# A software-pipelined transformer block: the second half's split moved into the next batch's feed-forward, the attention plan starting 16 slots ahead of it, 13 buffers in the ring, 12 filler matmuls a batch

## The reference

```
x = x + attention(layernorm(x))            # 8 heads of 16, two relative biases, causal mask over time
t = x                                      # residual for the feed-forward
n = layernorm(t)
p = softmax(n @ Wg); top = two largest, divided by their sum
for i in range(2):                         # both of the two weights
    w = n * top[..., i]
    h = gelu(einsum('btd,edf->ebtf', w, W1) + b1)
    out = out + einsum('ebtf,efd->btd', h, W2) + sum(b2)
x = t + out
```

## Time and profile before

| | |
|---|---|
| time, median of 3 runs | 2374.73 us (2370.79 to 2376.21) |
| the profiled execution | 2375.36 us |
| its span, from the first to the last instruction | 2373.6 us |
| TensorE busy (matmul) | 2212.2 us, 93% of the span |
| ScalarE busy | 1615.2 us, 68% |
| VectorE busy | 1309.2 us, 55% |
| GpSimd busy | 1063.1 us, 45% |
| mean granted clock of TensorE | 0.969 of 2.4 GHz |

### The profile page before, as it was taken

How to read it: one execution, slowest core, us unless ns; L and a number is a source line. 1 busy time by engine, 2 the same in 40 slices (tenths; PEclk the granted TensorE clock), 3 DMA queues, 4 the chain that set the end, 5 groups by cost and what they waited for, 6 DMA issues and landing times.

```text
span 2373.6 us, 48113 instructions
## 1 busy us (share of the span) xinstructions
PE 2212.2 (93%) x18213; PEld 2028.0 (85%) x18213; DVE 1309.2 (55%) x3191; ACT 1615.2 (68%) x2730; POOL 1063.1 (45%) x1051
## 2 busy tenths in 40 slices
PE   3779999999999999999998999999999999999998
PEld 2569898898988889898997988889898898988898
DVE  6246454755546466454755546466454755546453
ACT  2447677576776757677576776857677576776876
POOL 5124344443445344344443444344344443444366
PEclk7789999999999999999999999999999999999999
DMA  3412030220402212030220402212030220402200
GB/s 47 92 31 38 8 46 13 36 30 11 51 9 32 30 29 38 8 48 12 36 30 11 52 11 30 30 29 37 8 48 12 36 30 11 52 11 30 30 5 8
DMA packets 68528, 68.68 MB, mean 29 GB/s; under 512 B 20286, under 2 KB 53962, under 8 KB 68298
## 3 DMA queue, kind: packets, MB, share of 16 engines
q1 hardware_dynamic: 67634, 65.34, 19.4%
q10 hardware_dynamic: 664, 0.27, 0.0%
HBM read 10.83 MB, written 6.29 MB: 7 GB/s over the span
## 4 chain that ended last, share of the span: by engine, by line
PE 67%; DVE 17%; ACT 9%; issue 5%; POOL 1%; SPq 1%; DMA 0%; ACTq 0%; DVEq 0%; POOLq 0%
PE acc L925 20%; DVE maxes L682 7%; PE zps L914 6%; PE wide L857 6%; ACT z L535 6%; PE zps L916 6%; PE zps L915 6%; PE wide L845 5%; PE wide L828 4%; DVE h L745 3%; PE wide L871 2%; PE wide L879 2%; PE wide L864 2%; PE acc L902 2%; PE wide L811 1%
## 5 line engine op out<-in xcount | busy, mean ns | idle before, releaser
L469 POOL TENSOR_TENSOR h<-h 128x384 f32<-128x384 f32 x1024 | 1022.3, 1008 | 1236.3 <-ACT h L561 1225.6
L560 ACT ACTIVATE h<-zps,b_col 128x384 f32<-128x384 f32 x1024 | 591.6, 578 | 405.6 <-DVE h L745 346.7
L745 DVE TENSOR_TENSOR h<-zps,ratio_b 128x384 f32<-128x384 f32 x1024 | 542.3, 552 | 539.7 <-PE zps L916 528.5
L925 PE MATMUL acc<-w,h 128*128 128x128 f32 x6144 | 821.2, 277 | 0.2 <-DVE outt L754 0.2
L925 PEld LDWEIGHTS acc<-w,h 128*128 128x128 f32 x6144 | 800.5, 193 | 3.8 <-issue 0.5
L561 ACT ACTIVATE h<-h,b_col 128x384 f32<-128x384 f32 x1024 | 621.4, 607 | 0.0
L682 DVE TENSOR_REDUCE maxes<-wide 128x1 f32<-128x128 f32 (+5 forms) x768 | 430.2, 615 | 295.1 <-PE wide L828 293.6
L914 PE MATMUL zps<-x_hi,w_lo 128*128 128x384 f32 x1024 | 388.6, 379 | 11.5 <-ACT h L560 10.2
L535 ACT ACTIVATE z<-wide 128x896 f32<-128x896 f32 (+2 forms) x384 | 335.1, 916 | 33.9 <-PE wide L845 25.9
L915 PE MATMUL zps<-x_lo,w_hi 128*128 128x384 f32 x1024 | 347.9, 340 | 0.0
L916 PE MATMUL zps<-x_hi,w_hi 128*128 128x384 f32 x1024 | 347.1, 339 | 0.0
(11 more groups left out here) (99 smaller groups left out, 1469.3 us busy)
## 6 DMA issues: line engine op xcount, KB each, us to landing
stack<-halves SPq DMA_DIRECT2D x384, 96.0 KB, 3.1
stack<-halves SPq DMA_DIRECT2D x384, 24.0 KB, 2.6
out_dram<-outt SPq DMA_DIRECT2D x256, 24.0 KB, 1.6
x_in<-in_x SPq DMA_DIRECT2D x124, 48.0 KB, 2.4
stack<-max_rows SPq DMA_DIRECT2D x128, 3.0 KB
stack<-max_rows SPq DMA_DIRECT2D x128, 1.5 KB
w<-in_L_ffn_W SPq DMA_DIRECT2D x8, 256.0 KB, 4.0
stack<-z SPq DMA_DIRECT2D x2, 180.0 KB
```

What stands on the lines that cost most here:

```text
L469: pool.tensor_tensor(h1[:, PLACE[m], :], h0[:, m % 2, :], h1[:, PLACE[m], :], ALU.add).then_inc(hsum_ready, 1)
L560: act.activation(h0[:, m % 2, :], zps[BANK[m]][:, 0:CT], ACT.Gelu, bias=b1_col[:, j:j + 1]).then_inc(h0_ready, 1)
L745: vec.tensor_tensor(h1[:, PLACE[m], :], zps[BANK[m]][:, 0:CT], ratio_b[:, c * CT:(c + 1) * CT], ALU.mult).then_inc(z1_ready, 1)
L925: ins = pe.matmul(acc[:, n * P:(n + 1) * P], h1[:, PLACE[k], n * P:(n + 1) * P], w2[:, j, :], start=(j == 0 and n == 0), stop=(j == UNITS_ ...
```

## The change

The steps move earlier against the feed-forward, by 2.5 slots (the first scores) to 10.5 (the second group's first scores); the first, `stats`, goes from slot -6.5 to -16.5. So most steps stand elsewhere beside the units. The split of the second chunk is taken out of the list's end: the tokens of the second chunk are kept in a buffer of their own (`xn_last`), and their split is put at slot 15.5 of the batch that uses them, ahead of its second chunk's first unit. The ring `h1` has 13 places where it had 10; room for it comes from `mixed`, which now lies in `z`, and `outt`, which is gone (the sum is formed in `res`). The fillers are 2 and 4 at each group's first scores, and none at the split: 12 a batch. The first and the last batch get `FIRSTS` of their own, and the steps of batch 1 that would stand ahead of batch 0's slots are squeezed into its slots 0 to 9.5. The two heads of a pair share one block of ones in `val`, which makes it a quarter smaller.

```diff
-LAG = 4
-RING = 10
-FIRSTS = (2, 2, 1, 0, 1, 3, 0, 1, 2, 1, 2, 0, 2, 0, 2, 1, 0, 1, 1, 2, 0, 0, 0, 0, 0, 0, 0, 2, 3, 3, 0, 0,
-          1, 2, 1, 2, 2, 1, 0, 1, 3, 1, 0, 0, 0, 0, 2, 2, 3, 0, 1, 3, 1, 0, 0, 1, 0, 1, 0, 0, 0, 2, 0, 2)
+LAG = 5
+FIRST_LAG = 5
+KNOTS = ((-4.950000000000001, 3.0), (9.5, 9.5))
+RESIDUAL_AT = 14
+RING = 13
+FIRSTS = (2, 1, 1, 2, 2, 0, 1, 3, 1, 0, 2, 2, 0, 1, 2, 1, 0, 0, 0, 0, 0, 1, 2, 3, 1, 1, 1, 1, 1, 3, 1, 3,
+          0, 0, 0, 0, 0, 0, 2, 2, 3, 3, 1, 1, 0, 2, 0, 1, 1, 0, 0, 0, 0, 0, 0, 0, 0, 2, 0, 2, 1, 2, 1, 1)
...
-      ("split", 0): 60.0, ("split", 1): 60.0}
+AT = {("stats", 0): -16.5, ("seed", 0): -12.5, ("root", 0): -10.0, ("scale", 0): -7.0, ("turn", 0): -6.5, ("query", 0): -4.0,
+      ("key", 0): -4.0, ("value", 0): -2.5, ("rows", 0): 13.5, ("split", 1): 15.5, ("mix", 0): 23.0, ("sums", 0): 31.0,
...
                     for i in range(TILES):
-                        ins = vec.tensor_scalar(xn[:, i, :], xs[:, i, :], moments[:, 1, i, 0:1], ln_t[:, 1, i:i + 1],
+                        to = xn[:, i, :] if i < HT else xn_last[:, i - HT, :]
+                        ins = vec.tensor_scalar(to, xs[:, i, :], moments[:, 1, i, 0:1], ln_t[:, 1, i:i + 1],
                                                 ALU.subtract, ALU.mult)
...
+                if r.b > 0:
+                    vec.wait_ge(out_stored, r.at(16 * TPT * CHUNKS, 16 * (TPT * (c + 1 - CHUNKS) + 1)))
...
+                    if hh == 0 and part == 0 and (g == 1 or r.b > 0):
+                        n = WIDE["divide", 1 - g]
+                        act.wait_ge(wide_free[n % 2], r.at(WPB, n // 2 + 1 - (WPB if g == 0 else 0)))
...
                     if hh == 0 and part == 0:
-                        idle(w[:, 0:P], 3)
+                        idle(w[:, 0:P], 2)
...
                     if hh == 0 and part == 1:
-                        idle(acc[:, CT:CT + P], 5, start=False)
+                        idle(acc[:, CT:CT + P], 4, start=False)
...
                 elif step == "split":
-                    if a == 0:
-                        idle(w[:, 0:P], 8)
-                    pe.wait_ge(xn_ready, r.at(4, 3 + a))
+                    pe.wait_ge(weighed, Round(r.b - a).at(2, 1 + a))
```

More of the change, by code:

```diff
@@ new lines @@
+FIRSTS_LAST = (1, 1, 1, 1, 1, 1, 1, 1, 1, 1, 1, 1, 1, 1, 1, 1, 1, 1, 1, 1, 1, 1, 1, 1, 1, 1, 1, 1, 1, 1, 1, 1,
+          1, 1, 1, 1, 1, 1, 1, 1, 1, 1, 1, 1, 1, 1, 1, 1, 1, 1, 1, 1, 1, 1, 1, 1, 1, 1, 1, 0, 0, 0, 0, 0)
+RESIDUAL_AT = 14
+RING = 13
+FIRSTS = (2, 1, 1, 2, 2, 0, 1, 3, 1, 0, 2, 2, 0, 1, 2, 1, 0, 0, 0, 0, 0, 1, 2, 3, 1, 1, 1, 1, 1, 3, 1, 3,
+          0, 0, 0, 0, 0, 0, 2, 2, 3, 3, 1, 1, 0, 2, 0, 1, 1, 0, 0, 0, 0, 0, 0, 0, 0, 2, 0, 2, 1, 2, 1, 1)
+AT = {("stats", 0): -16.5, ("seed", 0): -12.5, ("root", 0): -10.0, ("scale", 0): -7.0, ("turn", 0): -6.5, ("query", 0): -4.0,
+      ("key", 0): -4.0, ("value", 0): -2.5, ("rows", 0): 13.5, ("split", 1): 15.5, ("mix", 0): 23.0, ("sums", 0): 31.0,
+      ("rows", 1): 31.0, ("divide", 0): 31.5, ("mix", 1): 38.5, ("sums", 1): 40.0, ("divide", 1): 41.0, ("project", 0): 41.5,
+      ("project", 1): 42.0, ("stats", 1): 43.0, ("seed", 1): 43.5, ("turn", 1): 45.0, ("root", 1): 45.0, ("gate", 0): 47.0,
+      ("weigh", 0): 54.0, ("split", 0): 54.5}
@@ L96 @@
 assert sum(FIRSTS) == UNITS
+assert sum(FIRSTS_ALONE) + FIRST_LAG == UNITS + LAG and sum(FIRSTS_LAST) + LAG == UNITS
 def places(count):
@@ L114, with squeezed @@
 BANK_BACK = back(BANK)
+def squeezed(slot):
+    x0, y0 = PLAN[0][0], 0.0
+    for x, y in KNOTS:
+        if slot < x:
+            return int(2 * (y0 + (slot - x0) * (y - y0) / (x - x0))) / 2
+        x0, y0 = x, y
+    return slot
 class Round:
@@ L262, in build, with rounds, run @@
         block = ctx.enter_context(nc.Block())
-        def rounds(eng, attention, unit, after, prepare=None):
+        def rounds(eng, attention, unit, after, prepare=None, skipped=None):
             first = Round(0)
+            def run(r, step, a):
+                due = r.b > 0 if (step, a) == ("split", 1) else r.b < BATCHES
+                if due:
+                    attention(r, step, a)
+                elif skipped and (step, a) in WIDE and WIDE[step, a] <= WIDE["split", 1]:
+                    skipped(r, step, a)
             for _, step, a in PLAN:
-                attention(first, step, a)
+                run(first, step, a)
                 if prepare:
                     prepare(first, step, a)
[L276 to L279, removed]
+            for m in range(FIRST_LAG):
                 unit(first, m)
@@ L302, in rounds @@
             for b in range(BATCHES):
-                slots(Round(b), Round(b + 1) if b + 1 < BATCHES else None, Round(b + 2) if b + 2 < BATCHES else None)
+                slots(Round(b), Round(b + 1), Round(b + 2))
         def wide_at(r, step, a):
@@ L927, in after @@
                 ins.then_inc(hsum_used, 1)
-            rounds(pe, attention, unit, after, prepare=prepare)
+            rounds(pe, attention, unit, after, prepare=prepare, skipped=skipped)
 WEIGHT_DMAS = 4
```

90 lines of the change are left out of this document (50 added, 40 removed).

## The result

| | median us | runs | ratio to before (95%) |
|---|---|---|---|
| before | 2375.47 | 2370.79 to 2377.47 | |
| after | 2266.49 | 2265.47 to 2268.63 | 0.9545 (0.9529 to 0.9562) |

The change takes 109 us. The forecast was 2250, its range 2220 to 2302. The profiled execution took 2266.91, its span is 2265.1 us where the earlier trace rows have 2373.6, so 108.5 us are to be explained.

What follows compares the result with a forecast made beforehand. TensorE's queue plus its waits was taken to bound the 142.2 us period. 7.2 + 2.9 - 1.9 = 8.2 us a batch, 123 over 15, and 4.9 at the end, less 3 at the start, gave 2250 us, range 2220 to 2302.

Steps and rivals of the forecast that it cites:

- The split: Between gate and split: 5.54 us of fillers and waiting go, plus 1.7 us of lowered clock; 7.2 us a batch.
- the first rival: Between gate and scale: VectorE, held by GpSimd, stays the bound; 1.5 to 3 us more, about 2285 us; chance 0.24.
- my own case: The forecast itself: gaps at split and scores closed, time within 15 us of 2250; chance 0.60.
- The new waits: TensorE waits newly at turn 1.2, query 0.3 and stack 0.4: 1.9 us a batch lost, bounds 0 and 6.
- The scores: Both groups' score stretches: 1.4 us from the first group's, 0.4 from fewer fillers, 1.1 less outside; 2.9 us a batch.
- The floor of 13.7: A group's stretch from first score tile to mix can't be shorter than about 13.7 us, however little TensorE has in it.
- The ends: Last feed-forward falls from 79.2 to 74.3 us, 4.9 less; the start costs 3 us more, between -6 and +12.
- signs of being right: Period 134 us, no idle above 0.5 us at split's transposes, clock 1.00, idle near 1 us at turn, L902's like only at scores.
- signs of being wrong: Split waiting 2 us or more, clock under 1 in scores, first scores over 15 us, stack wait, last feed-forward over 76.
- The slower rival: In the score stretches: with fewer fillers the clock falls to 1.2 GHz; about 2580 us; chance 0.04.
- Given back: Elsewhere in the batch: waits only move, so the time stays about as before, 2365 us or more; chance 0.04.
- all new waits vanish: At turn, query and stack: none of the 1.9 us a batch of waits appears; 2222 us; chance 0.08.

Runs made afterwards that it cites:

- ring10: The changed kernel with the ring of 10 places in place of 13, units that would lead by more moved to later slots; 2334.70 us, ratio 0.9838.
- fillers_none: The changed kernel without its 12 fillers (identity matmuls) a batch at the scores; 2253.86 us.

## Why the forecast was right, and where it was not

**The split** (7.2 forecast). The gap closed and the clock with it: 7.24 less the 0.63 left, 6.6. The 1.7 us for the clock had been read behind one split. In the 8 us behind each of the 14 splits that wait in the kernel before, the clock is 0.63 to 0.81, 0.74 in the mean, so it cost 2.1 us a batch, and what closed is 7.0.

VectorE took 823.60 - 816.74 = 6.9 us from the gate's maxima to the third weighed tile, where the forecast had 6.0. Among these are the two holds, (0.92 - 0.17) + (0.75 - 0.17) = 1.3 us, the first rival's mechanism at about half of its price of 2.3: by this sum VectorE would have been there first without them. The wait that they leave, 14 x 0.63 = 9 us, is a good part of the 16 us by which the forecast was low, and the measured 2266.5 lies just outside the 15 us of my own case and inside the 2265 to 2310 that I had given to the rival.

Of the skill's rule that I cited there (the Trainium skill, "SBUF — State Buffer", "SBUF: two separate sides") the runs agree in one more point: the operations held in the changed kernel's stretch have two SBUF inputs, and a multiplication that reads PSUM, at 818.36 beside GpSimd's first row, takes its usual 0.55. Other rows go further than what I cited: in `ring10` an operation with one input was held too, 0.81 us, and in the kernel before one at 716.36, 0.42 us, until GpSimd's operation of 715.76 had ended.

**The new waits** (1.9 forecast, 1.0 measured). The turn as forecast, 1.01 to 1.2; `query` and `stack`, 0.7 together, didn't wait.

**The scores** (2.9 forecast). Here the sum was mis-sized. The rest of the period's 7.42, 7.42 - 7.0 + 1.0 = 1.4 us, is all that scores, fillers and what else moved gave. The step that failed is "The first falls from 15.6 to about 14.2 (nearly balanced with ScalarE)": it became 16.4. The 14.2 doesn't even follow from the prediction's own prices. TensorE was full in that stretch, and two afters fewer, a unit and a maxima tile more are -1.34 + 0.60 + 0.55 = -0.2 us, the filler -0.2: 15.2. The rest are waits that the sum left out, 0.71 us for a buffer that ScalarE reads, and 0.4 between the first after (735.93) and the second tile (736.89), which the trace of `fillers_none` puts down to `x_lo` (0.58 there).

Where the time went is seen when the stretch is cut at the exponentials. The floor of 13.7 is, in the earlier trace rows, 2.4 us from the first tile to the first exponential, 10.75 of exponentials and 0.6 from the last one to the mix. In the changed first group these are 2.1, 11.1 and 3.1. Split 1's copies, which I suspected first, stand ahead of the table load and cost nothing against that floor; the fillers ahead of the third tile and `x_lo` ahead of the second cost 0.4, and in `fillers_none`, where the exponentials have no gap, the stretch is still 750.38 - 733.95 = 16.4. Nearly all of the excess stands behind the last tile: three maxima tiles, three units and two afters, so that the mix can't follow the exponentials. I had counted what stands beside the tiles, not where. That moving this work would bring the time isn't shown: no run took it all away from there, and the three that put one after more among the tiles gained nothing. The sentence that fillers inside the second group "lie beside ScalarE and give nothing" was wrong too: leaving out all 12 gives 1.2 us a batch.

**The ends.** The sum takes 8.2 us 15 times. The last of the 15 had no split to close: no next norm stands ahead of its `weigh`, and the last split of the kernel before doesn't wait (timeline of TensorE):

```profile
2280.28 1.95 PE L902 MATMUL wide<-ident 128*128 128x128 f32 x16
2282.06 0.27 PE L894 MATMUL wide<-ident,xn 128*128 128x128 f32 x1
```

From the last batch's first mix to slot 0 of the last feed-forward the kernel before takes 2288.56 - 2205.56 = 83.0 us, the changed one 2183.62 - 2100.74 = 82.9. The last feed-forward itself takes 2259.24 - 2183.62 = 75.6 from slot 0 to the last addition, where the earlier trace rows have 79.2: 3.6 of the forecast 4.9 (timelines of TensorE and VectorE in the changed kernel):

```profile
2183.62 0.42 PE L952 MATMUL zps<-x_hi,w_lo 128*128 128x384 f32 x1
2259.24 0.56 DVE L789 TENSOR_TENSOR res<-acc,res 128x384 f32<-128x384 f32 x1 [3.46 <-PE acc L963]
```

At the start, batch 0's second mix begins 6.9 us sooner than before (113.85, before 120.70), and the second batch's first mix only 0.9: the crowded early slots take back 6.0. The first split waits 3.02 us there, the turn of the second batch 4.73, `stack` 2.13, and from 133 to 143 us the clock is 0.50. For the fifteenth period and the start together the forecast was 8.2 - 3 = 5.2 us; they gave 0.9 + 0.1. So 14 x 0.8 = 11 us in the periods, 4.2 here and 1.3 in the last feed-forward make up the 16 us between 2250 and 2266.

Of the prediction's signs of being right all came but one, no idle time above 0.5 us at the split's transposes (0.63). Of its signs of being wrong one came: the first scores stretch over 15 us.

**The slower rival** (clock in the scores) is out: without any filler the clock is 1.00 in both stretches. The rule of "psum-queue depth-cycling" (the Trainium skill, "TensorE: Matmul & The Clock Gate") would have had it swing there; TensorE is busy for 16.25 of 18 and 12.18 of 13 us, and the measurement decides. **Given back** is out by the rows above, and so is **all new waits vanish**: the turn's 1.01 us stayed.

## What to carry to other kernels

Shift a serial chain under other work before removing parts of it: the second split alone brought nothing, and the fillers were only the visible part of a wait. When a stretch is set by two engines handing tiles back and forth through two buffers, count not only how much work stands in it but what stands directly ahead of each tile and behind the last; 0.6 us of TensorE work ahead of a long tile kept ScalarE idle for 0.38 us, and the same ahead of a short tile left its exponentials without a gap, though the time didn't fall by it. And a wait that one engine's chain causes is shortened on that engine; filling it with work of the waiting one moved it, and once made the kernel 21 us slower.

## What was unexpected of the hardware

A switch of ScalarE's table takes 1.28 us and the first exponential follows 0.02 us behind it (736.26, 737.56); it began 0.01 us behind the copy ahead of it. The Trainium skill ("ScalarE: Activation LUTs", "What ACT_TABLE_LOAD costs") has the same 1.28 and a drain of like length besides; no such drain shows here. And a hold of VectorE by GpSimd, 0.6 to 0.8 us on an operation of 0.17 in the stretches shown, is by its size four instructions of a norm: two of them are longer than the wait left at the split.
